# Sorting 20000 edges four columns at a time, with 16-bit operands and step marks

## The reference, cut to what matters

```python
edge_index = jnp.stack([src, dst])            # 20000 edges of 625 nodes
xl = (x @ W_l).reshape(N, HEADS, HEAD_DIM)    # 4 heads of 64
xr = (x @ W_r).reshape(N, HEADS, HEAD_DIM)
e = xl[src] + xr[dst]
e = jnp.where(e >= 0, e, NEG_SLOPE * e)       # 0.2
score = jnp.einsum('ehd,hd->eh', e, att)
m = jax.ops.segment_max(score, dst, num_segments=N)
ex = jnp.exp(score - m[dst])
alpha = ex / (jax.ops.segment_sum(ex, dst, num_segments=N)[dst] + SM_EPS)
agg = jax.ops.segment_sum(alpha[:, :, None] * xl[src], dst, num_segments=N)
```

## Time and profile before

| | us |
|---|---|
| median of 3 runs | 1215.3 |
| lowest and highest | 1213.15, 1218.66 |
| the profiled execution | 1216.8 |
| its span | 1215.0 |

### The profile page before, as it was taken

How to read it: one execution, slowest core, us unless ns; L and a number is a source line. 1 busy time by engine, 2 the same in 40 slices (tenths; PEclk the granted TensorE clock), 3 DMA queues, 4 the chain that set the end, 5 groups by cost and what they waited for, 6 DMA issues and landing times.

```text
span 1215.0 us, 20533 instructions
## 1 busy us (share of the span) xinstructions
PE 909.8 (75%) x5479; PEld 766.2 (63%) x5479; DVE 867.0 (71%) x2569; ACT 336.0 (28%) x1061; POOL 418.9 (34%) x401
## 2 busy tenths in 40 slices
PE   3958856586797788660373599998689489499996
PEld 2635535465686777660373599987468468398985
DVE  5179997777777777771488788866678964866645
ACT  0032213232443443342252111110136116121210
POOL 2049985444566666665000222214000000111104
PEclk9995557678798555675576599999789799699999
DMA  8720000000000000000970399997000000388893
GB/s 274 248 81 1 1 0 3 2 2 2 2 4 3 3 3 3 4 3 2 235 177 16 140 335 328 322 341 247 22 1 1 1 1 1 104 333 294 290 342 89
DMA packets 38293, 129.50 MB, mean 107 GB/s; under 512 B 12885, under 2 KB 20929, under 8 KB 29913
## 3 DMA queue, kind: packets, MB, share of 16 engines
q1 hardware_dynamic: 21742, 112.64, 28.1%
q0 software_dynamic: 10464, 8.67, 4.2%
q10 hardware_dynamic: 5992, 7.04, 1.6%
HBM read 108.83 MB, written 19.26 MB: 105 GB/s over the span
## 4 chain that ended last, share of the span: by engine, by line
PE 46%; DVE 27%; DMA 11%; issue 8%; POOL 3%; DVEq 2%; ACT 2%; POOLq 0%; ACTq 0%; SPq 0%
PE bank L794 12%; DVE mask_words L1086 7%; PE bank L805 6%; PE bank L585 5%; DMA arena<-pair_scores 4%; DMA pair_scores<-sc_ring,pair_cells 3%; PE bank L727 3%; POOL pair_scores L2120 2%; PE bank L490 2%; PE bank L548 2%; DVEq L1121 2%; PE bank L595 2%; PE bank L893 1%; PE bank L603 1%; PE bank L500 1%
## 5 line engine op out<-in xcount | busy, mean ns | idle before, releaser
L2120 POOL DMA_INDIRECT pair_scores<-sc_ring,pair_cells x184 | 225.0, 1223 | 171.4 <-issue 69.3
L2145 POOL DMA_INDIRECT arena<-row_tab,ids x42 | 57.6, 1371 | 496.3 <-DVE ids L1528 489.5
L585 PE MATMUL bank<-x_hi,hot 125*125 x368 | 144.4, 405 | 59.3 <-ACT tc L1879 37.0
L794 PE MATMUL bank<-arena 128*128 128x128 f32 x1480 | 182.3, 282 | 2.9 <-DMA arena<-in_exp 2.9
L794 PEld LDWEIGHTS bank<-arena 128*128 128x128 f32 x1480 | 176.9, 198 | 4.3 <-DMA arena<-in_exp 3.6
L585 PEld LDWEIGHTS bank<-x_hi,hot 125*125 125x125 f32 x368 | 96.3, 262 | 75.5 <-issue 74.2
L585 PE MATMUL bank<-x_lo,hot 125*125 x368 | 129.3, 362 | 0.0
L1869 ACT ACTIVATE hot<-bank 125x250 fp32r<-125x250 f32 x184 | 63.8, 379 | 228.0 <-PE bank L572 226.3
L2113 POOL TENSOR_SCALAR fmaps<-iota_c,tab 125x184 bf16<-125x184 f16 x120 | 96.3, 821 | 70.8 <-DVEq L1079 62.1
L1128 DVE TENSOR_TENSOR cnt<-cnt,bank 125x125 f32 x184 | 53.3, 290 | 69.1 <-issue 38.3
L585 PEld LDWEIGHTS bank<-x_lo,hot 125*125 125x125 f32 x368 | 99.1, 269 | 0.4
(11 more groups left out here) (381 smaller groups left out, 1756.6 us busy)
## 6 DMA issues: line engine op xcount, KB each, us to landing
arena<-in_exp SPq DMA_DIRECT2D x25, 1024.0 KB, 6.6
arena<-in_exp SPq DMA_DIRECT2D x17, 1386.0 KB, 6.3
arena<-in_exp0o SPq DMA_DIRECT2D x25, 512.0 KB, 6.7
pair_scores<-cnt SPq DMA_DIRECT2D x10, 1093.8 KB
arena<-in_exp1o SPq DMA_DIRECT2D x17, 640.0 KB
arena<-pair_scores SPq DMA_DIRECT2D x7, 1093.8 KB
slot_y<-arena ACTq DMA_DIRECT2D x34, 128.0 KB, 6.0
fmaps<-pair_scores SPq DMA_DIRECT2D x3, 1093.8 KB
```

The costliest lines, as they stand in the source:

```text
L585: mm = pe.matmul(banks[SUM_BANKS[(2 * i + c) % 3]][0:P, 0:ROW], hot[0:P, i % HOTS, c, w, :], part[:, bass.ds(rows[2 * c + w], ROW)], start ...
L794: mm = pe.matmul(banks[1 + 2 * q + buf][0:rows, i * SLOTS:(i + 1) * SLOTS], w_in(s, q, k, m, rows), xsT[:, s, k, :], start=(k == 0), stop= ...
L2120: p.indirect_dma_start(out=pair_scores[which], in_=sc_ring[:, i % SCORED, which, :], in_offset=None, out_offset=bass.IndirectOffsetOnAxis( ...
```

## The change

- Four columns (`GROUP`) are sorted per step, 40 steps. The chosen matrices are laid out with the column innermost (`[..., n, k]`), in a ring of 3 groups. Per group VectorE runs `mark_places` (`iota_4 == places16`, 125 x 500, 16-bit) one group ahead, and `choose_places` (the mark times `values16`, 125 x 1000, 16-bit).
- The second factor is no longer one-hot but a step: ScalarE makes sign(i - c + 0.5) for three columns of a group (the value is halved for them), POOL makes i >= c for the fourth. `read_nodes` takes differences of neighbouring columns.
- `slots_before` is split in two bf16 digits (`before16`), the selectors are bf16 (packed in the same input), and the membership matmul takes three buckets at once. The reduction over 25 buckets becomes a tree of additions.
- The layer norm moves before `copy_sums`; `owners` and `to_fm("xnT0")` move behind `slots` on TensorE; `copy_owners`, `from_fm`, the `lr` matmuls, their copies and the splits are done between sort steps (`SORT_STEPS`).
- The per-head sums come from weights multiplied by `att` (`weigh_weights`, `linear_heads`); `x_hi` is made by VectorE.
- In the pair loop the four one-hot matrices of a pair are one operation of 125 x 500, `weigh` one of 125 x 512, and the two counts of a pair stand apart. Registers are loaded for two blocks after the score, without bound checks, on TensorE one pair ahead. POOL waits for the scores once a pair.

```diff
-CHOSEN = 6
+GROUP = 4
+GROUPS = EC // GROUP
+CHOSEN = 3
+MARKS = SORTED + 1
+SORT_STEPS = {"turned": 1, "lr": 2, "weights": 4, "owners": 6, "linear": 8, "heads": 14, "rows": 18, "rows_lo": 20}
...
             def slots():
+                pe.wait_ge(sem("sorting"), SORTING["begun"])
                 for i, b in enumerate(range(0, BUCKETS, 3)):
                     after(pe, sem("slots_read"), i - 1)
-                    for q in range(b, min(b + 3, BUCKETS)):
-                        to = banks[3 + i % 2][0:P, (q - b) * EC:(q - b + 1) * EC]
-                        pe.matmul(to, before[:, :], member[:, q, :], start=True, stop=False)
-                        mm = pe.matmul(to, orders[:, q * P:(q + 1) * P], slots_before, start=False, stop=True)
+                    n = min(3, BUCKETS - b)
+                    bank = banks[3 + i % 2]
+                    pe.matmul(bank[0:P, 0:n * EC], before[:, :], member[:, b:b + n, :].rearrange("p b j -> p (b j)"),
+                              start=True, stop=False, skip_group_check=True)
+                    for q in range(b, b + n):
+                        for w in range(2):
+                            mm = pe.matmul(bank[0:P, (q - b) * EC:(q - b + 1) * EC], selectors[:, w, q, :],
+                                           before16[:, w, :], start=False, stop=True, skip_group_check=True)
                     mm.then_inc(sem("slots"), 1)
...
-                for j in range(EC):
-                    pe.wait_ge(sem("chosen"), j + 1)
...
+                pe.wait_ge(sem("chosen"), g + 1)
+                pe.wait_ge(sem("pool_columns"), g + 1)
+                for k in range(GROUP):
+                    if k < GROUP - 1:
+                        pe.wait_ge(sem("act_columns"), (GROUP - 1) * g + k + 1)
                     for w in range(2):
-                        mm = pe.matmul(banks[5 + w][0:P, 0:SORTED], chosen[:, j % CHOSEN, w, :],
-                                       columns16[:, j % CHOSEN, :], start=(j == 0), stop=(j == EC - 1))
-                    mm.then_inc(sem("placed"), 1)
+                        mm = pe.matmul(banks[5 + w][0:P, 0:MARKS], chosen[:, g % CHOSEN, w, :, k],
+                                       columns16[:, g % CHOSEN, k, 0:MARKS], start=(g == 0 and k == 0),
+                                       stop=(g == GROUPS - 1 and k == GROUP - 1))
+                mm.then_inc(sem("placed"), 1)
...
-                to_d, to_s = (onehot[:, c // 2 % TAKEN, c % 2, w, :] for w in range(2))
+                to_d, to_s = (onehot[:, c // 2 % TAKEN, :, c % 2 * 2 + w] for w in range(2))
...
-                own.link(v.tensor_reduce(slot_of, slot_parts.rearrange("p b j -> p j b"), AX.X, ALU.add))
+                flat = slot_parts.rearrange("p b j -> p (b j)")
+                for n in (12, 6, 3):
+                    own.link(v.tensor_tensor(flat[:, 0:n * EC], flat[:, 0:n * EC], flat[:, n * EC:2 * n * EC], ALU.add))
+                own.note(v.tensor_tensor(flat[:, 0:EC], flat[:, 0:EC], flat[:, 24 * EC:25 * EC], ALU.add))
+                own.link(v.tensor_tensor(flat[:, EC:2 * EC], flat[:, EC:2 * EC], flat[:, 2 * EC:3 * EC], ALU.add))
+                own.link(v.tensor_tensor(slot_of, flat[:, 0:EC], flat[:, EC:2 * EC], ALU.add))
...
-                for j in range(EC):
-                    after(dve, sem("placed"), j - CHOSEN + 1)
-                    for w in range(2):
-                        ins = v.tensor_scalar(chosen[:, j % CHOSEN, w, :], iota_c[:, 0:P], place_of[:, j:j + 1],
-                                              local[:, 1 - w, j:j + 1], ALU.is_equal, ALU.mult)
-                    ins.then_inc(sem("chosen"), 1)
+            def mark_places(g):
+
+                after(dve, sem("chosen"), g - 2)
+                own.note(v.tensor_tensor(placed16[:, g % 3, :, :], iota_4[:, :, :],
+                                         places16[:, GROUP * g:GROUP * (g + 1)].unsqueeze(1).to_broadcast([P, P, GROUP]),
+                                         ALU.is_equal))
+
+            def choose_places(g):
+
+                after(dve, sem("placed"), g - CHOSEN + 1)
+                dve.wait_ge(sem("dve_own"), marked[g])
+                v.tensor_tensor(chosen[:, g % CHOSEN, :, :, :],
+                                placed16[:, g % 3, :, :].unsqueeze(1).to_broadcast([P, 2, P, GROUP]),
+                                values16[:, :, GROUP * g:GROUP * (g + 1)].unsqueeze(2).to_broadcast([P, 2, P, GROUP]),
+                                ALU.mult).then_inc(sem("chosen"), 1)
...
-                for c in range(2):
-                    for w in range(2):
-                        ins = v.tensor_scalar(onehot[:, i % TAKEN, c, w, :], iota_1[:, :],
-                                              node_at[:, w, 2 * i + c:2 * i + c + 1], None, ALU.is_equal)
-                    ins.then_inc(sem("onehot"), 1)
...
+                v.tensor_tensor(onehot[:, i % TAKEN, :, :], iota_4[:, :, :],
+                                node_hot[:, 2 * i:2 * i + 2, :].rearrange("p c w -> p (c w)").unsqueeze(1)
+                                .to_broadcast([P, P, 4]), ALU.is_equal).then_inc(sem("onehot"), 1)
...
             for i in range(PAIRS):
                 if i + 2 < PAIRS:
                     make_hots(i + 2)
                 if i + 1 < PAIRS:
-                    add_counts(i + 1)
+                    add_counts(2 * i + 2)
+                weigh(i)
+                if i + 1 < PAIRS:
+                    add_counts(2 * i + 3)
                 score(i)
+                if i + 2 < PAIRS:
+                    load_counts(i + 2)
                 mix(i)
...
+            def mark_columns(g):
+
+                after(act, sem("placed"), g - CHOSEN + 1)
+                for k in range(GROUP - 1):
+                    j = GROUP * g + k
+                    a.activation(columns16[:, g % CHOSEN, k, 0:MARKS], iota_c[:, :], ACT.Sign, bias=column_bias[:, j:j + 1])\
+                        .then_inc(sem("act_columns"), 1)
...
-                pool.wait_ge(sem("scored"), i + 1)
+                if which == 0:
+                    pool.wait_ge(sem("scored"), i + 1)
```

295 lines of the change are left out of this document (180 added, 115 removed).

## The result

The changed kernel takes 1117.95 us (median; 1111.0 to 1120.35) beside 1214.22 us (1209.76 to 1218.66) for the kernel before on the same chip: a ratio of 0.920, 95% interval 0.914 to 0.925. The forecast was 1115, the range 1093 to 1145. The profiled span is 1117.8 us, 97.2 shorter.

What follows compares the result with a forecast made beforehand. No one engine bounds the whole; four stages before the score table's fetch were read separately, VectorE pacing the sort, POOL the later pairs. Gains 34 + 50 + 1 + 15 = 100 take 1216.8 to 1117, median 1115; range 1093 to 1145.

Steps and rivals of the forecast that it cites:

- Stage A: Finding each edge's slot, 0 to 71.0 us, before the sort; forecast to end at 37, gain 34, bounds 27 and 36.
- Stage B: The sort, until the sorted nodes are read; forecast from 107.3 to 57 us, gain 50, bounds 23 and 60.
- Stage C: Short operations between the sorted nodes being read and the first scatter, 12.0 us; forecast gain 1.
- Stage D: The 92 pairs to the last scatter's end; gain 15, bounds 0 and 36; S(i) is pair i's scatter start.
- (4): Slots' matmuls: per three buckets one 480-column and six 160-column bf16 matmuls; nine rounds 7 to 14 us, 8 taken.
- (3): Making `before16` ahead of the slots: five VectorE operations of 0.2, 1.0 us, counted in the slots' start at 23.
- Rival (a): Sort: the 16-bit two-tensor form runs at the fp32 rate, 27 us later, total 1142; chance 0.17.
- (f): Pair loop: VectorE's two-tensor forms slow POOL's scatters; 1.19 us at both places read, so given nothing of its own.
- Rival (e): Sort and pairs: TensorE's stationary loads at 8-byte step slow; gain gone at 0.33 us per load, 1353 at 0.5; chance 0.03.
- Rival (b): Sort: TensorE stays at half clock though loaded, about 78 us for the sort, total 1136; chance 0.12.
- Rival (c): The pairs gain more, 21 us at most, and the sort nears 50 us; total about 1095; chance 0.13.
- rival (d): Pair loop: POOL limits the pairs so fully that only the earlier start is gained; total 1130; chance 0.05.

Runs made afterwards that it cites:

- experiment 1: Changed kernel with only the slots' matmuls as before (fp32 `orders` rows, three membership matmuls, no digits or casts for them): 1132.0 us, ratio 0.931.
- (2): Kernel before with only the pair loop's part of the change added: 1190.5 us, ratio 0.980.
- Experiment 6: Changed kernel with the choice's second operand read from fp32 words instead of 16-bit ones: 1131.8 us, ratio 0.931.
- experiments 7 and 8: Changed kernel with eight more matmuls per sort group, their stationary operand strided (7), 1148.4 us, or dense (8), 1136.1 us.
- experiment 3: Changed kernel with registers loaded as before, eight at every fourth pair on VectorE, with bound checks, TensorE's also moved back: 1140.1 us, ratio 0.938.
- experiment 4: Changed kernel with the dense branch's steps spread, from pair 6 on one at every second pair: 1099.0 us, ratio 0.905.

## Why the prediction was right, and where it wasn't

The total is 3 us off because errors of both signs met: A +6.5, B +3, C -1, D -6.6 against the forecast stages, where the forecast span was 1115. That they nearly cancel is luck. Two pieces are shown by undoing or adding them alone, the slots' matmuls (experiment 1) and the whole of the pair loop (2). The moved layer norm, the tree and the sort's parts (groups of four, step marks, woven `lr`) were read from rows and not undone one by one.

**Stage A: +6.5.** The start of the slots at 23 held (23.05), and so did the tree (5.0 us, forecast 4.6) and the 1.6 behind it. The term that failed is (4): nine rounds in 8 us took 13.8. I had both ends, 7 and 14, and chose the low one "since the clock is full throughout this stage". They ran at 1.2 columns per ns, as the two widths of L566 show, and a round took 1.57 us, by the forecast's own sum 1.5 at half clock. The 1.00 in the earlier trace rows that it leaned on was for its first 5 us no reading: the first clock entry of the kernel before is at 76.01. Edits (3) and (4) together were worth 14.1 us (experiment 1), and stage A 27.5 in all, near the lower bound of 27.

**Stage B: +3.** The forms cost less than forecast: 0.33 + 0.59 = 0.92 per group against 1.0, and POOL's marks add 0.14 to that against 0.15, which was right. VectorE's sum came to 50.4 us (19.3 + 31.0) against 56. The Trainium skill's tier table ("VectorE: DVE Perf Modes") gives `tensor_tensor` on 16-bit data twice the pace of fp32, and the trace agrees: 500 elements more take 0.26 us, 1.9 per ns, where fp32 ones run at 0.91 (L1206, 2560 in 2.81 us). Experiment 6 shows the price of leaving that tier, 0.52 us per 1000 elements. Rival (a) was thus false; its 27 us were a fair price, since one of the two operations alone, with two thirds of the elements, cost 14 to 16.

What failed is the overlap. I compared VectorE's sum with TensorE's sum for the whole stage and took the larger. Each was the late one in a part of its own, and VectorE was idle for 9.8 of the 60.2 us, against 1 in the forecast. For 7.2 of them, up to 70 us, TensorE was the late one, where `lr` is woven in (one group and four `lr` matmuls 2.64 us, 50.52 to 53.16); 2.14 are the wait for the last sums.

"POOL 40 operations of 0.82, 33 us. Both are hidden" held in that nothing is seen to wait for POOL, but the 0.82 didn't: a mark took 1.08 in the steady part. In (f) I had asked only about the scatters and read 1.19 us at two places. Pair 40's takes 2.25 in the changed kernel and 2.04 in the one before, so VectorE does slow some of them. What the Trainium skill says of shared interfaces ("GPSIMD Engine Reference", section 1), that POOL contends with VectorE's instructions of two SBUF inputs or in a 2-port perf mode, is borne out for two inputs by marks of 3.49 us and this scatter. The mark of 2.15 us beside a cast of one tensor would be the 2-port case; no view shows the mode.

**Rival (e)** had the right mechanism and a harmless size: a strided load costs 0.117 us with its matmul against 0.083 (experiments 7 and 8), far from the 0.33 from which it decides, but more than the 0.095 in my sum. The Trainium skill's sentence that two hits per 16-byte line keep full bandwidth ("SBUF — State Buffer", "Door 1: The DMA port swizzle") is not borne out by TensorE's loads here. **Rival (b)** held for the first 5 us of the sort; later stretches at the lower level (0.66 in 80 to 90 us) made VectorE wait for TensorE by 0.4 us.

**Stage C** gained 2.2 us instead of 1.

**Stage D: -6.6.** The form of the argument held: the end is the largest S(i) + (92 - i) x POOL's pace, and the place is pair 39 or 40. At pair 24 the gain was 124.7 - 105.6 = 19.0 us, not 12; at pair 39 it was 184.1 - 166.6 = 17.5, not 15.6; and behind it POOL's own pace improved from 3.80 to 3.67, 4.1 us over the rest, which I had put at nothing. The registers didn't bring that: with them loaded as before POOL's pace is 3.69 too ((494.65 - 306.47)/51). Which of the other edits did stays open. The mis-sized term is the registers: 0.46 of loads "hidden behind the reduction", in a sum of 1.2 of which "only 0.5 is realised". They alone are 0.70 per pair up to pair 24 (experiment 3). The pairs' floor by POOL was forecast as a bound (36 us of gain) and is real, but lies lower: experiment 4 reached it, with 338.9 us instead of 384.0. Rival (c), that the pairs gain more, was thus partly true (6.6 us of its 21), and rival (d), that only the earlier start counts, was false.

## What to carry to other kernels

Where two engines share a stage, add up the later one of each part, not the larger of two sums. An engine that paces a long queue at constant speed turns everything late in its feed into loss: find the last pair at which it still waits, and thin out what fills the feeding engine ahead of that pair (here 19 us). Work that is hidden on POOL can still cost VectorE time: count its operations times what each adds (0.14 us here). Before you take a granted clock of 1.00 as a reading, check it by the starts of one line at two widths.
